# Router logits of an expert-mixture kernel: turned by VectorE in 32 x 32 squares instead of by TensorE

## What is computed

```python
q_emb = relu(cond @ W3 + b3)                       # one row for each sequence
h = relu(((64 * x + sum_over_tokens(x)) * q_emb) @ W2 + b2)
logits = h @ gate_w.T                              # 64 experts
scores = softmax(logits); topk_w, topk_i = top_k(scores, 6)
# each expert takes its first 64 tokens in token order
y = sum over a token's experts of topk_w * (silu(t @ w_gate) * (t @ w_up)) @ w_down
shared = silu(h @ sw_gate) * (h @ sw_up) @ sw_down # 704 wide
out = x + y + shared
```

## Time and profile before

| | before |
|---|---|
| median of 3 runs | 1238.36 us |
| the profiled execution's own time | 1238.84 us |
| its span, first to last instruction | 1237.0 us |
| TensorE busy, matmuls | 1223.1 us, 99% |
| TensorE weight loads (beside the matmuls) | 905.8 us, 73% |
| VectorE busy | 741.7 us, 60% |
| ScalarE busy | 333.2 us, 27% |
| GpSimd busy | 272.4 us, 22% |
| mean granted TensorE clock | 0.994 |
| read from and written to memory | 197.14 and 61.10 MB |

### The profile page before, as it was taken

How to read it: one execution, slowest core, us unless ns; L and a number is a source line. 1 busy time by engine, 2 the same in 40 slices (tenths; PEclk the granted TensorE clock), 3 DMA queues, 4 the chain that set the end, 5 groups by cost and what they waited for, 6 DMA issues and landing times.

```text
span 1237.0 us, 15789 instructions
## 1 busy us (share of the span) xinstructions
PE 1223.1 (99%) x5892; PEld 905.8 (73%) x5892; DVE 741.7 (60%) x1405; ACT 333.2 (27%) x632; POOL 272.4 (22%) x246
## 2 busy tenths in 40 slices
PE   8999999999999999999989999999999999999998
PEld 8888888888888888888756666666666666666666
DVE  6898989989888898877424234343333423423332
ACT  3654243434324443433111111110111201111110
POOL 0000000000000000000424355353552543545420
PEclk9999999999999999999989999999999999999999
DMA  9947444372644537058556987988979899899862
GB/s 185 232 121 189 96 132 115 90 183 48 182 94 126 122 90 181 16 152 282 158 191 234 329 270 262 350 265 277 337 233 321 302 273 300 284 286 309 273 144 78
DMA packets 159821, 250.91 MB, mean 203 GB/s; under 512 B 23616, under 2 KB 94400, under 8 KB 158592
## 3 DMA queue, kind: packets, MB, share of 16 engines
q1 hardware_dynamic: 143968, 223.66, 57.2%
q0 software_dynamic: 14048, 25.18, 10.0%
q10 hardware_dynamic: 1728, 1.05, 0.3%
HBM read 197.14 MB, written 61.10 MB: 209 GB/s over the span
## 4 chain that ended last, share of the span: by engine, by line
PE 93%; DVE 5%; issue 1%; DMA 1%; SPq 0%; ACT 0%; ACTq 0%
PE bank L1394 23%; PE bank L1396 22%; PE bank L1395 22%; PE bank L1594 12%; PE bank L1617 7%; PE bank L1513 1%; PE bank L1512 1%; PE bank L1450 1%; PE bank L1448 1%; PE bank L1603 1%; DMA x<-in_x_dram 1%; DVE x L882 1%; DVE xpart L886 1%; PE bank L1461 0%; DVE x L899 0%
## 5 line engine op out<-in xcount | busy, mean ns | idle before, releaser
L1394 PE MATMUL bank<-hh,gu 128*128 128x512 f32 x704 | 281.7, 400 | 3.0 <-issue 2.9
L1396 PE MATMUL bank<-hh,gu 128*128 128x512 f32 x704 | 275.7, 392 | 0.9 <-issue 0.8
L1395 PE MATMUL bank<-hl,gu 128*128 128x512 f32 x704 | 275.5, 391 | 0.9 <-issue 0.8
L590 POOL DMA_INDIRECT hg<-table,idx_quarter x128 | 127.1, 993 | 637.7 <-DVE idx_hi L1284 599.0
L1394 PEld LDWEIGHTS bank<-hh,gu 128*128 128x128 f32 x704 | 132.8, 189 | 40.1 <-issue 14.5
L1396 PEld LDWEIGHTS bank<-hh,gu 128*128 128x128 f32 x704 | 132.8, 189 | 30.0 <-issue 1.5
L1395 PEld LDWEIGHTS bank<-hl,gu 128*128 128x128 f32 x704 | 133.1, 189 | 29.3 <-issue 3.6
L650 ACT ACTIVATE ah<-prod 128x512 fp32r<-128x512 f32 x96 | 60.6, 632 | 303.1 <-DVE prod L949 285.7
L949 DVE TENSOR_TENSOR prod<-bank,prod 128x512 f32<-128x512 f32 x96 | 66.1, 688 | 125.4 <-PE bank L1396 108.8
L1394 PE MATMUL bank<-sdh,ah 128*128 128x512 f32 x320 | 126.8, 396 | 0.0
L1396 PE MATMUL bank<-sdh,al 128*128 128x512 f32 x320 | 124.7, 390 | 0.0
(11 more groups left out here) (128 smaller groups left out, 1676.5 us busy)
## 6 DMA issues: line engine op xcount, KB each, us to landing
wg<-in_L_ffn_w_gate_dram SPq DMA_DIRECT2D x64, 704.0 KB
wu<-in_L_ffn_w_up_dram SPq DMA_DIRECT2D x64, 704.0 KB
wd<-in_L_ffn_w_down_dram SPq DMA_DIRECT2D x64, 512.0 KB
table<-hrow SPq DMA_DIRECT2D x64, 256.0 KB, 4.3
x<-in_x_dram SPq DMA_DIRECT2D x60, 256.0 KB, 6.9
wd<-in_L_ffn_w_down_dram SPq DMA_DIRECT2D x64, 192.0 KB
out_dram<-outst SPq DMA_DIRECT2D x36, 256.0 KB
outst<-in_x_dram SPq DMA_DIRECT2D x32, 256.0 KB, 3.5
```

Source lines behind the costliest of these rows:

```text
L590: nc.gpsimd.indirect_dma_start(out=hg[p % 3][:, b, :], out_offset=None, in_=quarters, in_offset=bass.IndirectOffsetOnAxis(ap=idx_quarter[: ...
L1394: nc.tensor.matmul(o, st_h, mv_h, start=first_mm, stop=False)
L1395: nc.tensor.matmul(o, st_h, mv_l, start=False, stop=False)
L1396: return nc.tensor.matmul(o, st_l, mv_h, start=False, stop=last_mm)
```

## The change

Three things change.

1. `take_lraw` no longer copies the bank as it lies. Sixteen copies of 32 partitions x (4 x 32) move it block by block: the 32 x 32 block of experts h and tokens a goes to the token block's partitions a and the expert block's columns h, once for the high part and once for the low. `lsb` becomes [128, 2, 4, 64].
2. A new `fold(n)` on VectorE adds the two parts into `lg`, and `route` begins with one stream transpose of `lg` (128 x 256) in place, which turns each 32 x 32 square. TensorE's `logits`, ScalarE's `take_low`, the bank for turned logits and their semaphores go, with the waits on `z_ready` that kept that bank. In pass 0 `take_lraw(b)` stands where `take_low(b)` stood; in the other passes it stays ahead of the first silu.
3. In the second stage `("rows", 0, 0)` comes after tile 0 instead of tile 1, so VectorE turns the first pair's rows ahead of its product of tile 1.

```diff
-        lsb = keep("lsb", [P, CH])
+        lsb = keep("lsb", [P, 2, J, E])
...
-                    if v == ND and n == 1:
+                    if v == ND and n == 0:
                         yield "rows", 0, 0
...
-            sp.wait_ge(s.logits_filled, NCH)
+            sp.wait_ge(s.lsum_ready, NCH)
             load_gate(1)
...
             def take_lraw(n):
                 act.wait_ge(s.lraw_filled, n + 1)
-                wait(act, s.logits_filled, n)
-                copy(lsb[:, :], lraw_bank(n)[:, :]).then_inc(s.lraw_taken, 1)
-
-            def take_low(n):
-
-                act.wait_ge(s.logits_filled, n + 1)
-                wait(act, s.z_ready, n)
-                parts = logits_bank(n)[:, :].rearrange("p (j h e) -> p h j e", j=J, h=2)
-                copy(lg[:, :, :], parts[:, 1, :, :]).then_inc(s.llow_ready, 1)
+                wait(act, s.lsum_ready, n)
+
+                for part in range(2):
+                    for a in range(P // SQ):
+                        for h in range(E // SQ):
+                            cols = slice(h * SQ, (h + 1) * SQ)
+                            blocks = lraw_bank(n)[part * E + h * SQ:part * E + (h + 1) * SQ, :].rearrange(
+                                "p (j a i) -> p a j i", j=J, i=SQ)
+                            op = copy(lsb[a * SQ:(a + 1) * SQ, part, :, cols], blocks[:, a, :, :])
+                op.then_inc(s.lraw_taken, 1)
...
                 for oc in range(KC):
                     take_cond(b, oc)
-                    if i > 0 and oc == 0:
-                        take_low(a)
...
-                take_lraw(b)
+                if i > 0:
+                    take_lraw(b)
                 if i == 0:
                     split_piece(4)
-                    take_low(a)
...
                 silu(v, 0)
-                if i > 0:
-                    take_low(b)
                 split_a(v, 0)
...
                 silu(v, 3)
                 if i == 0:
                     split_xm(c, 1)
-                    take_low(b)
+                    take_lraw(b)
                 split_a(v, 3)
...
+            def fold(n):
+                dve.wait_ge(s.lraw_taken, n + 1)
+                nc.vector.tensor_tensor(lg[:, :, :], lsb[:, 0, :, :], lsb[:, 1, :, :], ALU.add).then_inc(s.lsum_ready, 1)
+
             def route(n):
-
-                parts = logits_bank(n)[:, :].rearrange("p (j h e) -> p h j e", j=J, h=2)
-                dve.wait_ge(s.llow_ready, n + 1)
-                link(nc.vector.tensor_tensor(lg[:, :, :], parts[:, 0, :, :], lg[:, :, :], ALU.add))
+                dve.wait_ge(s.lsum_ready, n + 1)
+                squares = lg[:, :, :].rearrange("p j e -> p (j e)")
+                link(nc.vector.transpose(squares, squares))
...
                     split_h(b, oc)
+                    if i == 0 and oc == 0:
+                        fold(a)
...
+                    fold(b)
                     route(b)
                     product(v, 0)
...
                     take_rows(c, 2)
+                    fold(c)
                     merge_drop(*m[6])
...
                 product(v, 4)
+                fold(b)
                 route(b)
                 mark(b)
...
                 take_down(v, 1)
+                fold(c)
                 take_down(v, 2)
 
             def last_half(i):
                 b, v = 2 * i + 1, i
+                fold(b)
                 route(b)
...
-                if oc == 2:
-                    pe.wait_ge(s.z_ready, n if n % 2 == 0 else n - 1)
...
-            def logits(n):
-                pe.wait_ge(s.lraw_taken, n + 1)
...
-                for j in range(J):
-                    op = nc.tensor.transpose(logits_bank(n)[:, j * P:(j + 1) * P], lsb[:, j * P:(j + 1) * P],
-                                             ident[:, :])
-                op.then_inc(s.logits_filled, 1)
...
                 if i > 0:
-                    cond_tile(b, 0)
-                    logits(a)
-                    for oc in range(1, KC):
+                    for oc in range(KC):
                         cond_tile(b, oc)
                     down_tile(v - 1, 3)
-                else:
-                    logits(a)
                 logits_raw(b)
                 for t in range(GT):
                     gu_tile(v, t)
-                    if t == (2 if i == 0 else 0):
-                        logits(b)
```

More of the change, by code:

```diff
@@ L234, in adaln_moe_ffn_kernel @@
             lraw_taken = sem("lraw_taken")
-            logits_filled = sem("logits_filled")
-            llow_ready = sem("llow_ready")
+            lsum_ready = sem("lsum_ready")
             route_step = sem("route_step")
@@ L350, in lraw_bank @@
             return bank[7 if n == 0 else 5]
-        def logits_bank(n):
-            return bank[7] if n == 0 else bank[3] if n % 2 == 0 else bank[6]
         def second_stage():
```

## The result

| | before | after |
|---|---|---|
| median of 16 runs each, by turns on one chip | 1237.92 us (1236.95 to 1238.44) | 1241.07 us (1239.14 to 1242.42) |
| the profiled execution's own time | 1238.84 us | 1240.33 us |
| its span | 1237.0 us | 1238.5 us |

The ratio is 1.0024, with a 95% interval of 1.0017 to 1.0031: **slower by about 3 us**, where 4.05 us less had been forecast. 1241.07 lies 0.6 us above the upper end of the range, 1240.5, within the time of rival (b).

A forecast was written before the change was run, and what follows sets the result against it. TensorE was taken as the bound (93% of the chain). Transposes -6.3, first pass +2.75 and rows -0.5 sum to -4.05 us: 1238.84 becomes 1234.8, and with the runs' median 0.48 lower 1234.3 us; range 1230 to 1240.5.

The forecast's parts named there:

- (b): Rival: ScalarE doesn't overlap such small copies at all, with the clock loss on top; 1239 to 1242 us; chance 0.12.
- Part 1: Transposes leave TensorE: four a chunk cost 0.45 us, so chunks 2 to 15 give 6.3 us.
- Part 2: Sixteen copies on ScalarE at 0.16 us each take 2.56 us, hidden from the second pass on; upper end 0.26 a copy.
- Part 3: VectorE's new transpose in `route` takes 0.45 us with hand-over, 0.9 a pass; VectorE doesn't bound passes 1 to 7.
- Part 4: First pass: copies and chunk 1's transpose make VectorE, then TensorE, 2.75 us late at chunk 2's raw logits.
- Part 5: First pair's rows turned earlier, ahead of the expert matmuls: 0.5 us won if gathered data are there by 609.5, else 0.
- (a): Rival: the clock falls in TensorE's new first-pass hole, costing 1.6 to 4.7 us: 1235.9 to 1239; chance 0.14.
- (c): Rival: a copy on ScalarE costs 0.2 to 0.26 us and the clock holds; 1235 to 1237.1 us; chance 0.12.
- (d): Rival: TensorE's stall near 620 us goes or shifts; if freed, the time falls to 1225; chance 0.08.
- (e): Rival: VectorE bounds passes 1 to 7 after all and its waits only move; near 1238 us; chance 0.06.

The follow-up runs named there:

- c3_last_shared: c2_both_late with, in the last pass, VectorE making the eight copies of the low part while ScalarE makes the high part's; 1221.70 us, 0.9939 of the kernel before.
- a5_four: Changed kernel with each block left in its quarter, four copies in a row to a quarter (logits wrong); 1225.75 us against 1229.43 before, ratio 0.9971.
- c1_b_early: Changed kernel with chunk 1's sixteen copies right behind the first silu of pass 0; 1235.34 us, 0.9978 of before; on the other chip 1226.01 us, 0.9971.
- c2_both_late: Changed kernel with, in pass 0, chunk 0's copies behind the first silu and chunk 1's in two lots behind the third and fourth; 1223.25 us, 0.9952 of before.
- c5_rows_back: c3_last_shared with the first pair's rows turned behind the product of tile 1 again; 1222.77 us, 0.9946 of the kernel before.
- halfz: Copy form in a test kernel that computes nothing of the reference: ScalarE copies from PSUM, always on the low 64 partitions; 0.171 us a copy.
- half: Copy form in the same kind of test kernel: ScalarE copies from PSUM on 64 partitions, low and high by turns; 0.283 us a copy.
- m1_forms: Test kernel computing nothing of the reference: nine forms of PSUM copy back to back on ScalarE, then two on VectorE; the change's own form took 0.279 us a copy.
- a1_rows_back: Changed kernel with the first pair's rows turned behind the product of tile 1 again; 1240.77 us, 1.0019 of the kernel before.

## Why the prediction was wrong

- **Part 1, right.** 0.45 us a chunk was forecast and 0.483 measured over 12 chunks, with 438.00 of 438 us busy from 112 to 550. By that the 14 chunks give 6.8 us instead of 6.3.
- **Part 2 is the step that failed**: "I take 0.16, since copies do overlap in these rows". A copy of 0.268 us came every 0.281, nothing overlapped, and the stated upper end of 0.26 was still too low. The rows that it went by are copies over all 128 partitions with neighbours over all 128. For that kind the line through them (0.14) and the 0.16 taken are near: 0.156 was measured for 128 elements. But the new copies change partitions each time, and none of the rows showed such a pair. The forecast had named this sign: copies 0.25 us or more apart. What it said of the other passes held: nothing is lost from 112 to 550 us, and no wait stands ahead of `route(a)`. It did not ask this of the last pass, where `fold` has no other work ahead of it. At 0.281 that cost VectorE 4.12 us of waiting. TensorE waited 1.24 us, and from chunk 15's raw logits to the ranks it took 9.78 us where `c3_last_shared` takes 8.40: 1.4 us.
- **Part 3, right.** The transpose of 128 x 256 takes 0.45 us (0.42, or 0.45 with its hand-over, was forecast), and VectorE bounds none of the middle passes.
- **Part 4: mechanism, place and formula right, and its size wrong with the copy.** With 4.49 us for 16, the split behind chunk 1's copies is 4.49 - 0.26 = 4.23 late, the transpose adds 0.45, and chunk 0's copies exceed their slack of 2.96 by 1.53: 6.21 us, where TensorE was 6.27 late. `a5_four` checks the formula at a second pace (3.33 and 3.40), and `c1_b_early` and `c2_both_late` the place.
- **Part 5, right on its condition.** 0.5 us was forecast if the gathered rows are there in time; the trace after shows 0.55, those of `c3_last_shared` and `c5_rows_back` 0.56. In `c2_both_late` the rows came too late, and it gave nothing. On the first chip it isn't seen in the total, where the stall differs by more from one execution to the next.
- **The rivals.** It came out as (b), given 0.12: no overlap, with the clock's loss of (a), here 1.6 us, on top. Its 1239 to 1242 holds the 1241.07, by other sizes than it named: it asked for a copy of 0.26 us with the long clock loss of 4.7, and what came was 0.281, the short loss, and 1.4 us of the last pass, which no case had and which the range lacked. So that its range fits is partly luck. (a)'s mechanism is shown too, but its hole is 6 us, not 2.75. (c), 0.2 to 0.26 us a copy, just misses. (d): the stall stayed; from the first pair's to the second pair's first matmuls 28.32 us became 27.88. (e) is out.
- **The sum with the measured terms** is -6.8 + 6.27 + 1.6 + 1.4 - 0.55 = +1.9 us, as far as the experts' start. The times say +2.0 (0.5 to 2.7 by the interval) on the second chip, which agrees, and +3.15 (2.1 to 3.8) on the first. The two profiled executions there differ by 1.49 us. What makes the rest of the 3.15 is not shown; the stall is where single executions differ most.

## What to carry to other kernels

Price a small copy by neighbours that change partitions as it does: rows of whole-bank copies say nothing of quarter copies that hop. Work that leaves the bounding engine must go where the receiving engine is idle, in every pass; the same 16 copies at two other places in ScalarE's list, and 8 of them given to the engine that waits in the last pass, made 0.9939 out of 1.0013 on one chip. A chain without slack passes each microsecond on, so look at the first and last passes by themselves before trusting the middle.

## What was not expected of the hardware

- On ScalarE a copy from PSUM overlaps the one before it by about 0.11 us only if both its source and its destination lie on the same partitions as that one's (0.158 against 0.279 us for 32 x 128 elements from PSUM; 0.171 against 0.283 for 64 partitions, `halfz` and `half`). VectorE seems to do the same: 0.198 us a copy over 128 partitions, 0.30 over 32 where the quarter changes. No run has VectorE copy 32 partitions that stay, so that the change and not the width does it is not shown there. In the trace of `m1_forms`, where the first group lasts from 83.41 to 86.58:

```profile
83.41 3.26 DVE L79 COPY vw<-bank 128x128 f32<-128x128 f32 x16 [32.39 <-ACT z4x L88]
86.58 4.78 DVE L79 COPY vq4x<-bank 32x128 f32<-32x128 f32 x16
```

- One kernel took 1238.1 us on one chip and 1229.4 on another. Most of the difference lies in one stretch of some 20 us. On the first chip the profile puts TensorE's idle time there down to `issue` and 9.31 us of ScalarE's in before to `remote`, neither of which names a cause.
- Behind the same hole near 102 us the granted clock fell in the execution of after (0.90 over 17 us, which is 3.4 us at the lower level) and not in that of `a1_rows_back` (1.00).
